# Two accumulators for the scattered expert outputs of a sixteen-image network, instead of one

## The chip, the cores and the metric

The kernel runs on one core of one Trainium2 chip. The core has five engines that work in parallel and wait for each other by semaphores: TensorE (PE in the profile, with its weight loads as PEld), VectorE (DVE), ScalarE (ACT), GpSimd (POOL) and SyncE (SP). SP, ACT and POOL also start transfers (DMAs), which all run on the same 16 DMA engines. The metric is the device time of one execution in microseconds (us), as the median of several runs.

## What is computed

A batch of 16 images of 128 channels and 32x32 pixels goes through a chain of blocks (a convolution block, linear attention, two attention layers, two feed-forward layers). The change is in the last one, a mixture of eight experts. There `x` is seen as 16,384 tokens of 128 channels. Eight rounds of row and column normalising give each token a gate for each expert; each of the 8 experts takes its best `m` = 128 tokens, multiplies them by its 128x128 matrix, and the results are added back at the places of the tokens:

```python
vals, idx = jax.lax.top_k(jnp.transpose(cg, (0, 2, 1)), m)      # 128 of 16384 tokens per expert
...
routed = xf[jnp.arange(h)[:, None, None], idx]
outputs = jnp.einsum('hmei,eio->hmeo', routed, experts)
outputs = outputs * gate_values[..., None]
...
s = jnp.zeros((N, o_dim), srcf.dtype).at[idxf].add(srcf)
c = jnp.zeros((N,), srcf.dtype).at[idxf].add(1.0)
return s / (c + 1.0)[:, None]
...
t = t + _L3_ffn_ref(_ln_t(t), L3_ffn_gate_w, L3_ffn_experts)
```

Two experts can choose the same token, so the additions of different experts to one row must not run over each other.

## The kernel before

The activations stay in the core's memory as `X`, 128 channels (partitions) by 16,384 tokens. The network is a row of phases, with a barrier of all engines after each. Two phases touch the change.

`phase_route` finds the tokens. Its SP part fills the accumulator `res` in device memory (16,384 rows of 128 float32, 8 MB) with zeros: 8 DMAs of 1 MB (line 2252), written `(t p) c -> p t c`, so that one partition of a DMA holds 16 rows that lie 128 rows apart, 512 bytes each. VectorE works through the routing in one chain of dependent steps; near its end line 2444 makes `ids`, the token number of each of the 128 picks of each expert (`tile_of * 128 + tok`). The zeros need only be there at the barrier after the phase.

`phase_experts` has four parts.

- Gather: POOL fetches the tokens of each expert with one indirect DMA each (line 2474, 8 DMAs).
- Experts: PE transposes them (line 2502) and multiplies by the expert's matrix (line 2507); VectorE scales each result by its weight into `give[:, e, :]` (line 2527, counted by `o_saved`).
- Scatter: POOL adds `give[:, e, :]` into the rows of `res` with an indirect DMA that accumulates (line 2481). Each waits for the landing of the one before (`added`, line 2480), since two experts may share a row.
- Read-back: SP waits for all eight scatters (line 2487), then loads `res` image by image (1,024 tokens, 512 KB, line 2492) into `rows[u]`, two buffers `u`. PE turns each 128x128 piece with a transpose into the banks `px[u][h]` (8 per image, line 2515), VectorE adds each half image to `X` (line 2533), and ACT writes the image to the output (line 2541). SP may load image b once the transposes of image b - 2 are done (`x_mm`, line 2491).

The helper `over` runs the 16 images as two straight steps, a loop, and two straight steps. Each engine issues its instructions in the order of the code; nothing reorders them.

Of the kernel before, what the change touches and what calls it, by code (L numbers as in the profile page):

```python
# [11 lines left out]
F32 = mybir.dt.float32  # L12
BF16 = mybir.dt.bfloat16
ALU = mybir.AluOpType
# [3 lines left out]
C = 128  # L18
B = 16
HW = 32  # L20
N = HW * HW
T = B * N
# [390 lines left out]
def wait_if(eng, sem, value):  # L413

    if not isinstance(value, int) or value > 0:
        eng.wait_ge(sem, value)
# [1748 lines left out]
E8 = 8  # L2165
ITERS = 8
TOP = N // E8
NT = T // C
CLIP = 1e-10


def phase_route(nc, K, D, Y, ids, ws):

# [3 lines left out]
    with Mem(nc, "sk") as m:  # L2179
# [63 lines left out]
        with nc.Block() as block:  # L2243
            @block.sync
            def _(sp):
                sp.wait_ge(const_ready, 1)
                for j in range(4):
                    sp.dma_start(gw[:, j, 32 * j:32 * j + E8], D["gate_w"]).then_inc(g_in, 16)

                sp.wait_ge(const_ready, 2)  # L2250
                for k in range(NT // 16):
                    sp.dma_start(D["res"][k * 16 * C:(k + 1) * 16 * C, :].rearrange("(t p) c -> p t c", p=C),
                                 zeros[:, :, :]).then_inc(zero_out, 16)
                sp.wait_ge(zero_out, 16 * (NT // 16))

            @block.gpsimd
            def _(g):
# [84 lines left out]
            def _(v):  # L2342
# [98 lines left out]
                for k in range(4):  # L2441
                    step(v.tensor_tensor(sel[:, 2 * k:2 * k + 2, :], pair[k][:, :, 0, :], bc_n(rank[:, 2 * k:2 * k + 2]), ALU.is_le))
                step(v.reduce_sum(tok[:, :], sel[:, :, :], AX.X))
                step(v.scalar_tensor_tensor(ids[:, :], tile_of[:, :], float(C), tok[:, :], ALU.mult, ALU.add))
                step(v.tensor_tensor(sel[:, :, :], token[:, :].rearrange("p (o n) -> p o n", o=1).to_broadcast([C, E8, C]),
                                     bc_n(tok[:, :]), ALU.is_equal))
                for k in range(4):
# [1 line left out]
                step(v.reduce_sum(ws[:, :], sel[:, :, :], AX.X))  # L2449


def phase_experts(nc, K, D, X, ids, ws):


    TI = N // C
    with Mem(nc, "ex") as m:
        ew = m.sb("ew", [C, E8, C])
        got = m.sb("got", [C, E8, C])
        gotT = m.sb("gotT", [C, E8, C])
        give = m.sb("give", [C, E8, C])  # L2460
        rows = [m.sb(f"rows{u}", [C, TI, C]) for u in range(2)]
        pt = [m.ps(f"pt{u}", [C, C]) for u in range(2)]
        po = [m.ps(f"po{u}", [C, C]) for u in range(2)]
        px = [[m.ps(f"px{u}{h}", [C, 4, C]) for h in range(2)] for u in range(2)]
        e_in, got_in = m.sem("e_in"), m.sem("got_in")
        t_ready, t_saved, o_mm, o_saved, added = (m.sem(x) for x in ("t_ready", "t_saved", "o_mm", "o_saved", "added"))
        rows_in = [m.sem("rows_in0"), m.sem("rows_in1")]
        out = [m.sem("out0"), m.sem("out1")]
        x_mm, x_ready = m.sem("x_mm"), m.sem("x_ready")
        with nc.Block() as block:  # L2470
            @block.gpsimd
            def _(g):
                for e in range(E8):
                    g.indirect_dma_start(got[:, e, :], None, D["tokens"], bass.IndirectOffsetOnAxis(ap=ids[:, e:e + 1], axis=0))\  # L2474
                     .then_inc(got_in, 16)
                for e in range(E8):
                    g.wait_ge(o_saved, e + 1)
                    if e:

                        g.wait_ge(added, 16 * e)  # L2480
                    g.indirect_dma_start(D["res"], bass.IndirectOffsetOnAxis(ap=ids[:, e:e + 1], axis=0), give[:, e, :], None,
                                         compute_op=ALU.add).then_inc(added, 16)

            @block.sync
            def _(sp):
                sp.dma_start(ew[:, :, :], D["experts"]).then_inc(e_in, 16)
                sp.wait_ge(added, 16 * E8)

                def step(b, u, last):

                    wait_if(sp, x_mm, 2 * b - 2)
                    sp.dma_start(rows[u][:, :, :], D["res"][bass.ds(b * N, N), :].rearrange("(t p) c -> p t c", p=C))\  # L2492
                      .then_inc(rows_in[u], 16)

                over(sp, B, step)

            @block.tensor
            def _(pe):
                for e in range(E8):
                    pe.wait_ge(got_in, 16 * E8)  # L2500
                    wait_if(pe, t_saved, e - 1)
                    pe.transpose(pt[e % 2][:, :], got[:, e, :], K["ident"][:, :]).then_inc(t_ready, 1)  # L2502
                pe.wait_ge(e_in, 16)
                for e in range(E8):
                    pe.wait_ge(t_saved, e + 1)
                    wait_if(pe, o_saved, e - 1)
                    pe.matmul(po[e % 2][:, :], gotT[:, e, :], ew[:, e, :], start=True, stop=True).then_inc(o_mm, 1)  # L2507

                def step(b, u, last):
                    pe.wait_ge(rows_in[u], 8 * (b - u) + 16)  # L2510
                    for h in range(2):

                        wait_if(pe, x_ready, 2 * b + h - 3)
                        for r in range(4):
                            done = pe.transpose(px[u][h][:, r, :], rows[u][:, 4 * h + r, :], K["ident"][:, :])  # L2515
                        done.then_inc(x_mm, 1)

                over(pe, B, step)

            @block.vector  # L2520
            def _(v):
                for e in range(E8):
                    v.wait_ge(t_ready, e + 1)
                    v.tensor_copy(gotT[:, e, :], pt[e % 2][:, :]).then_inc(t_saved, 1)  # L2524
                for e in range(E8):
                    v.wait_ge(o_mm, e + 1)
                    v.tensor_scalar(give[:, e, :], po[e % 2][:, :], ws[:, e:e + 1], None, ALU.mult).then_inc(o_saved, 1)  # L2527

                def step(b, u, last):
                    for h in range(2):  # L2530
                        v.wait_ge(x_mm, 2 * b + h + 1)
                        xb = X[:, bass.ds(b * N + h * CH, CH)]
                        v.tensor_tensor(xb, xb, px[u][h][:, :, :].rearrange("p r c -> p (r c)"), ALU.add).then_inc(x_ready, 1)  # L2533

                over(v, B, step)

            @block.scalar
            def _(a):
                def step(b, u, last):
                    a.wait_ge(x_ready, 2 * b + 2)  # L2540
                    a.dma_start(D["out"][bass.ds(b, 1)].rearrange("o c n -> c (o n)"), X[:, bass.ds(b * N, N)]).then_inc(out[u], 16)

                over(a, B, step)
                for u in range(2):
                    a.wait_ge(out[u], 16 * B // 2)


def build(nc, D):
    with ExitStack() as ctx:
        def sb(name, shape, dt=F32):  # L2550
            return ctx.enter_context(nc.sbuf_tensor(name, shape, dt))

        K = {"ident": sb("ident", [C, C]), "ones": sb("ones", [C, C]),
             "neghalf": sb("neghalf", [C, C]), "mask8": sb("mask8", [C, C]),
             "eps": sb("eps", [C, 4]), "negone": sb("negone", [C, 4]),
             "stats": sb("bnstats", [C, NCH, 6])}
        X = sb("X", [C, T])
        D["proj"] = nc.dram_tensor("proj", [C, T], F32).ap()
        D["qk"] = nc.dram_tensor("qk", [2, 3, C, T], BF16).ap()
        D["tokens"] = nc.dram_tensor("tokens", [T, C], F32).ap()  # L2560
        D["res"] = nc.dram_tensor("res", [T, C], F32).ap()
        D["u"] = nc.dram_tensor("u", [C, T // C, C + RVW], F32).ap()
        phase_constants(nc, K)
        phase_conv(nc, K, D, X)
        phase_linatt(nc, K, D, X)
        phase_linatt_norm(nc, K, D, X)
        phase_attn_prep(nc, K, D, X)
        phase_attn(nc, K, D, X)
        with Mem(nc, "ffn") as m:
            Y = m.sb("Y", [C, T])  # L2570
            wcol, b2w = m.sb("wcol", [C, FT, B]), m.sb("b2w", [C, B])
            phase_norm(nc, K, X, Y, "n2")
            phase_router(nc, K, D, Y, wcol, b2w)
            phase_ffn(nc, K, D, X, Y, wcol, b2w)
        with Mem(nc, "gqa") as m:
            Y = m.sb("Y", [C, T])
            phase_norm(nc, K, X, Y, "n3")
            phase_gqa(nc, K, D, X, Y)
        with Mem(nc, "moe") as m:
            Y = m.sb("Y", [C, T])  # L2580
            ids, ws = m.sb("ids", [C, E8], mybir.dt.int32), m.sb("ws", [C, E8])
            phase_norm(nc, K, X, Y, "n4", D["tokens"])
            phase_route(nc, K, D, Y, ids, ws)
            phase_experts(nc, K, D, X, ids, ws)


def layout(inputs):
# [59 lines left out]
```

## Time and profile before

| | us |
|---|---|
| median of 3 runs | 5307.86 (5302.34 to 5311.43) |
| the profiled execution, its own time | 5307.08 |
| its span in the trace | 5305.1 |
| first scatter starts | 5206.79 |
| last scatter landed, first load of `res` issued | 5238.73 |
| last addition to `X` ends | 5301.42 |
| end of the span | 5305.1 |

So the scatters take 31.9 us and the read-back with the output takes 66.4 us, both at the very end of the program, where nothing else runs beside them. Starts are in microseconds from the start of the span. A row of the timeline shows the start, the duration, the engine, the line, what is written and read, how many instructions are merged in the row, and in brackets how long the engine was idle before it and what ended that. A row of the windows view shows the stretch, its length, the busy time of PE, PEld, DVE, ACT and POOL with the number of their instructions, and then PEclk, the granted clock of TensorE, 1.00 for 2.4 GHz and 0.50 for 1.2 GHz; the last two are the mean busy share of the 16 DMA engines and what they moved in GB/s.

### The profile page before, as it was taken

Reading aid. Unit: us, or ns where it says so; the run is one execution under the profiler, and the core shown is the slowest. Engines: PE = TensorE matmul, PEld = TensorE weight load, DVE = VectorE, ACT = ScalarE, POOL = GpSimd, SP = SyncE. Lnnn points to the kernel's source line nnn. Section 1 sums busy time; section 2 is a strip of 40 time slices with the busy share of each in tenths; the row PEclk is TensorE's granted clock in tenths of the full one; section 3 lists DMA queues with packets and bytes.
Section 4 is the critical chain, followed back from the end, with each engine's and each line's share of the span. In section 5 each row is a group of like instructions: output and inputs, shape, how many; then the busy total and the mean of one; then the engine's idle time right before and its main releaser. Section 6 shows DMA issues by size and latency. Waiting matters only on the chain. (4 is left out here: it accounts for less than half of the span.)

```text
span 5305.1 us, 72474 instructions
## 1 busy us (share of the span) xinstructions
PE 4422.0 (83%) x21774; PEld 1678.8 (32%) x21775; DVE 3041.7 (57%) x5454; ACT 2105.6 (40%) x3845; POOL 1822.3 (34%) x1328
## 2 busy tenths in 40 slices
PE   5499999994699999999999999966999999565323
PEld 2133333332422222222222222223444444344222
DVE  4777777774687776767676677634000000567562
ACT  3311111114626665656565566653443344413100
POOL 1000000003727776767676777771000000303001
PEclk9799999996969999999999999987999999866655
DMA  1343344434722222322222222010000000213204
GB/s 68 73 101 88 88 103 95 90 69 159 257 37 30 32 32 30 41 31 30 31 36 31 37 31 32 7 48 35 0 0 0 0 0 0 99 44 124 78 0 138
DMA packets 208215, 295.49 MB, mean 56 GB/s; under 512 B 43943, under 2 KB 136109, under 8 KB 206525
## 3 DMA queue, kind: packets, MB, share of 16 engines
q1 hardware_dynamic: 179768, 256.87, 21.9%
q10 hardware_dynamic: 23808, 25.17, 1.3%
q0 software_dynamic: 4368, 10.07, 0.6%
q8 instruction: 142, 2.33, 0.2%
q14 instruction: 129, 1.06, 0.1%
HBM read 94.49 MB, written 69.73 MB: 31 GB/s over the span
## 5 line engine op out<-in xcount | busy, mean ns | idle before, releaser
L1578 DVE TENSOR_REDUCE at_mx<-at_side 128x1 f32<-128x512 f32 x2048 | 1295.0, 684 | 415.1 <-PE at_side L1481 404.2
L1652 ACT ACTIVATE at_P<-at_S 128x512 f32<-128x512 f32 x2048 | 1120.2, 599 | 749.5 <-PE at_S L1513 698.1
L1411 POOL TENSOR_TENSOR at_pairs<-at_P 128x2048 f32<-128x2048 f32 x256 | 1160.3, 4533 | 316.1 <-ACT at_P L1652 295.5
L1513 PE MATMUL at_S<-at_qo,at_ko 99*128 99x512 bf16 x2048 | 784.2, 387 | 76.0 <-ACT at_P L1652 76.0
L1481 PE MATMUL at_side<-at_ko,at_qo 96*128 96x512 bf16 x2048 | 788.8, 398 | 44.0 <-DMA at_ko<-qk 23.3
L1929 ACT ACTIVATE ff_hs<-ff_ph,ff_b 128x512 f32<-128x512 f32 x512 | 351.6, 687 | 524.0 <-PE ff_ph L1899 524.0
L1524 PE MATMUL at_num<-at_P,at_rvt 128*32 128x512 f32 x4096 | 550.1, 609 | 0.0
L1899 PE MATMUL ff_ph<-ffn_Y,ff_w 128*128 (+1 forms) x1024 | 524.3, 594 | 8.7 <-DMA ff_b<-in_b_dram 8.7
L1913 PE MATMUL ff_po<-ff_hs,ff_w2s 128*128 128x512 f32 x1024 | 522.5, 592 | 0.0
L616 PE MATMUL la_acc<-la_rep,la_wagg 128*32 128x512 f32 x4096 | 511.1, 606 | 1.2 <-DMA la_rep<-la_pad 1.2
L773 DVE SCALAR_TENSOR_TENSOR la_dwq<-la_pad,la_taps,la_dwq 128x1024 f32<-128x1024 f32 x384 | 491.7, 1280 | 7.2
L1948 DVE SCALAR_TENSOR_TENSOR X<-ff_po,ffn_b2w,X 128x512 f32 (+1 forms) x32 | 24.0, 751 | 822.3 <-PE ff_po L1913 822.3
L1513 PEld LDWEIGHTS at_S<-at_qo,at_ko 99*128 99x128 bf16 x2048 | 196.1, 97 | 884.0 <-ACT at_P L1652 684.2
L1008 POOL TENSOR_TENSOR n_ln_ab<-n_ln_mv,eps 128x4 f32<-128x4 f32 x96 | 19.1, 199 | 1201.8 <-DVE n_ln_mv L999 1199.9
L587 POOL DMA_DIRECT2D proj<-la_y x32 | 17.4, 543 | 993.5 <-ACT la_y L847 993.5
L1481 PEld LDWEIGHTS at_side<-at_ko,at_qo 96*128 96x128 bf16 x2048 | 201.3, 98 | 325.3 <-DVE at_mx L1578 136.5
L1535 PE MATMUL at_den<-at_pairs,ones 128*32 128x512 f32 x2048 | 277.1, 613 | 7.7 <-POOL at_pairs L1411 7.6
L1899 PEld LDWEIGHTS ff_ph<-ffn_Y,ff_w 128*128 128x128 f32 x1024 | 195.1, 191 | 254.2 <-issue 244.9
L1913 PEld LDWEIGHTS ff_po<-ff_hs,ff_w2s 128*128 128x128 f32 x1024 | 194.5, 190 | 245.0 <-issue 244.4
L1023 ACT ACTIVATE n_ln_xt<-n_ln_front,n_ln_ab 128x128 f32<-128x128 f32 x384 | 144.6, 456 | 102.7 <-POOL n_ln_ab L1014 92.1
L616 PEld LDWEIGHTS la_acc<-la_rep,la_wagg 128*32 128x32 f32 x4096 | 105.8, 108 | 246.5 <-issue 228.1
L831 ACT COPY la_agg<-la_acc 128x512 f32<-128x512 f32 x64 | 37.5, 587 | 343.1 <-PE la_acc L616 343.1
(409 smaller groups left out, 4601.0 us busy)
## 6 DMA issues: line engine op xcount, KB each, us to landing
la_rep<-la_pad SPq DMA_DIRECT2D x512, 162.2 KB, 3.6
qk<-ap_part SPq DMA_DIRECT2D x32, 768.0 KB, 3.7
at_qo<-qk SPq DMA_DIRECT2D x192, 128.0 KB, 4.6
at_ko<-qk SPq DMA_DIRECT2D x192, 128.0 KB, 7.7
n_ln_xs<-X SPq DMA_DIRECT2D x96, 256.0 KB, 2.3
u<-ap_us SPq DMA_DIRECT2D x32, 320.0 KB, 4.0
X<-in_x_dram SPq DMA_DIRECT2D x4, 2048.0 KB, 22.1
proj<-la_y POOLq DMA_DIRECT2D x32, 256.0 KB, 2.3
```

The costliest lines, as they stand in the source:

```text
L616: last = pe.matmul(acc[h][32 * j:32 * j + 32, :], wagg[:, p - 1, j, g, :], view[:, :, 0:HW], start=(g == 0), stop=(g == NG - 1))
L773: v.scalar_tensor_tensor(out, image, taps[:, t:t + 1], out, ALU.mult, ALU.add).then_inc(tap_done, 1)
L1411: g.tensor_tensor(pairs[i % 2][:, :, :], P[a][:, :, :], P[a + 1][:, :, :], ALU.add).then_inc(pair_done, 1)
L1481: return pe.matmul(side[bank][:, :], qo[1 - u][0:KQ, s, i * C:(i + 1) * C], ko[1 - u][0:KQ, s, h * CH:(h + 1) * CH], start=True, stop=True)
L1513: pe.matmul(S[n % RING][:, :], ko[u][:, h, j * C:(j + 1) * C], qo[u][:, h, half * CH:(half + 1) * CH], start=True, stop=True).then_inc(s_r ...
L1524: last = pe.matmul(num[32 * i:32 * i + 32, :], rvt[u][:, j, :], P[k % SLOTS][:, i, :], start=(j == 0), stop=(j == 7))
L1535: last = pe.matmul(den[32 * i:32 * i + 32, :], K["ones"][:, 0:32], pairs[(k // 2 - 1) % 2][:, i, :], start=(j == 0), stop=(j == 6))
L1578: v.reduce_max(mx[:, n // 2, n % 2:n % 2 + 1], side[bank][:, :], AX.X).then_inc(side_saved, 1)
L1652: a.activation(P[k % SLOTS][:, i, :], S[(4 * k + i) % RING][:, :], ACT.Exp).then_inc(p_ready, 1)
L1899: pe.matmul(ph[j % R][:, :], w1[:, f, :], Y[:, bass.ds(b * N + half * CH, CH)], start=True, stop=True).then_inc(h_mm, 1)
L1913: done = pe.matmul(po[half][:, :], w2s[u][:, f, :], hs[j % R][:, :], start=(f == 0), stop=(f == FT - 1)).then_inc(h_used, 1)
L1929: a.activation(hs[j % R][:, :], ph[j % R][:, :], ACT.Gelu, bias=b1[:, j % FT:j % FT + 1]).then_inc(h_ready, 1)
```

## The change

There are now two accumulators, `res` for the experts 0, 2, 4, 6 and `res1` for 1, 3, 5, 7. A scatter waits for the one two before it, on the same accumulator (`added[0]` and `added[1]`). Both accumulators are zeroed. The rows are laid out in another order in memory: token `tile * 128 + tok` lies in row `tok * 128 + tile`, so that the rows that one partition loads for an image (8 tiles) or zeroes in one DMA (16 tiles) lie side by side, 4 KB and 8 KB. VectorE makes these row numbers (`places`) with one more instruction. In the read-back both accumulators are loaded, transposed and added to `X`: per image two loads, 16 transposes and 4 additions where there were one, 8 and 2. There are still four banks `px`, now one for each accumulator and half image, so that they hold one image where they held two.

```diff
             for k in range(NT // 16):
-                sp.dma_start(D["res"][k * 16 * C:(k + 1) * 16 * C, :].rearrange("(t p) c -> p t c", p=C),
-                             zeros[:, :, :]).then_inc(zero_out, 16)
-            sp.wait_ge(zero_out, 16 * (NT // 16))
+                for chain in ("res", "res1"):
+                    sp.dma_start(D[chain].rearrange("(p t) c -> p t c", p=C)[:, 16 * k:16 * k + 16, :],
+                                 zeros[:, :, :]).then_inc(zero_out, 16)
+            sp.wait_ge(zero_out, 32 * (NT // 16))
...
             step(v.scalar_tensor_tensor(ids[:, :], tile_of[:, :], float(C), tok[:, :], ALU.mult, ALU.add))
+            step(v.scalar_tensor_tensor(places[:, :], tok[:, :], float(NT), tile_of[:, :], ALU.mult, ALU.add))
...
-        rows = [m.sb(f"rows{u}", [C, TI, C]) for u in range(2)]
+        rows = [[m.sb(f"rows{k}{u}", [C, TI, C]) for u in range(2)] for k in range(2)]
-        px = [[m.ps(f"px{u}{h}", [C, 4, C]) for h in range(2)] for u in range(2)]
+        px = [[m.ps(f"px{k}{h}", [C, 4, C]) for h in range(2)] for k in range(2)]
...
                 for e in range(E8):
                     g.wait_ge(o_saved, e + 1)
-                    if e:
-                        g.wait_ge(added, 16 * e)
-                    g.indirect_dma_start(D["res"], bass.IndirectOffsetOnAxis(ap=ids[:, e:e + 1], axis=0), give[:, e, :], None,
-                                         compute_op=ALU.add).then_inc(added, 16)
+                    if e >= 2:
+                        g.wait_ge(added[e % 2], 16 * (e // 2))
+                    g.indirect_dma_start(chains[e % 2], bass.IndirectOffsetOnAxis(ap=places[:, e:e + 1], axis=0), give[:, e, :], None,
+                                         compute_op=ALU.add).then_inc(added[e % 2], 16)
...
-                    wait_if(sp, x_mm, 2 * b - 2)
-                    sp.dma_start(rows[u][:, :, :], D["res"][bass.ds(b * N, N), :].rearrange("(t p) c -> p t c", p=C))\
-                      .then_inc(rows_in[u], 16)
+                    wait_if(sp, x_mm, 4 * b - 4)
+                    for k in range(2):
+                        sp.dma_start(rows[k][u][:, :, :], chains[k].rearrange("(p t) c -> p t c", p=C)[:, bass.ds(b * TI, TI), :])\
+                          .then_inc(rows_in[u], 16)
...
-                    pe.wait_ge(rows_in[u], 8 * (b - u) + 16)
+                    pe.wait_ge(rows_in[u], 16 * (b - u) + 32)
                     for h in range(2):
-                        wait_if(pe, x_ready, 2 * b + h - 3)
-                        for r in range(4):
-                            done = pe.transpose(px[u][h][:, r, :], rows[u][:, 4 * h + r, :], K["ident"][:, :])
-                        done.then_inc(x_mm, 1)
+                        for k in range(2):
+                            wait_if(pe, x_ready, 4 * b + 2 * h + k - 3)
+                            for r in range(4):
+                                done = pe.transpose(px[k][h][:, r, :], rows[k][u][:, 4 * h + r, :], K["ident"][:, :])
+                            done.then_inc(x_mm, 1)
...
                     for h in range(2):
-                        v.wait_ge(x_mm, 2 * b + h + 1)
                         xb = X[:, bass.ds(b * N + h * CH, CH)]
-                        v.tensor_tensor(xb, xb, px[u][h][:, :, :].rearrange("p r c -> p (r c)"), ALU.add).then_inc(x_ready, 1)
+                        for k in range(2):
+                            v.wait_ge(x_mm, 4 * b + 2 * h + k + 1)
+                            if k:
+                                v.wait_ge(x_ready, 4 * b + 2 * h + 1)
+                            v.tensor_tensor(xb, xb, px[k][h][:, :, :].rearrange("p r c -> p (r c)"), ALU.add).then_inc(x_ready, 1)
```

On POOL, at the gathers and scatters in `phase_experts`, the instructions stand as follows (semaphore names in brackets are those of the first phase that used the same semaphore: `conv_pool` is `o_saved`, `conv_vec` is `added` before and `added[0]` after, `conv_act` is `added[1]`):

```order
-L2474 DMA ex_got<-tokens,moe_ids 128x128 x8
-L2481 DMA res<-ex_give,moe_ids 16384x128 [waits conv_pool]
-L2481 DMA res<-ex_give,moe_ids 16384x128 [waits conv_vec,conv_pool] x7
...
+L2478 DMA ex_got<-tokens,moe_ids 128x128 x8
+L2485 DMA res<-ex_give,moe_places 16384x128 [waits conv_pool] x2
+L2485 DMA res<-ex_give,moe_places 16384x128 [waits conv_vec,conv_pool]
+L2485 DMA res<-ex_give,moe_places 16384x128 [waits conv_act,conv_pool]
```

The second scatter no longer waits for the first, and from the third on the waits alternate between the two semaphores; the eight are still issued by one engine, one after the other.

On PE, inside the loop of the read-back, one image (of the two in the loop's body) stands as follows (`conv_pe` and `conv_coef1_ready` are the landings of the loads, `conv_v1_ready` before and `conv_v2_ready` after are `x_ready`, the additions that free a bank):

```order
 L416 ISA [waits conv_pe]
-L2515 MATMUL ex_px<-ident,ex_rows 128x128 [waits conv_v1_ready]
-L2515 MATMUL ex_px<-ident,ex_rows 128x128 x3
-L416 REGISTER_ALU
-L2515 MATMUL ex_px<-ident,ex_rows 128x128 [waits conv_v1_ready]
-L2515 MATMUL ex_px<-ident,ex_rows 128x128 x3
+L2522 MATMUL ex_px<-ident,ex_rows 128x128 [waits conv_v2_ready]
+L2522 MATMUL ex_px<-ident,ex_rows 128x128 x3
+L416 REGISTER_ALU
+L2522 MATMUL ex_px<-ident,ex_rows 128x128 [waits conv_v2_ready]
+L2522 MATMUL ex_px<-ident,ex_rows 128x128 x3
+L416 REGISTER_ALU
```

Two groups of four transposes have become four groups, each with its wait for a bank, behind one wait for both loads of the image.

## Rows read from the trace of the kernel before

**Rows 1.** The timeline: first two scatters, the last, and the loads of `res`.

```profile
5206.79 1.63 POOL L2481 DMA_INDIRECT res<-ex_give,moe_ids  x1 [6.20 <-DVE ex_give L2527]
5211.02 1.56 POOL L2481 DMA_INDIRECT res<-ex_give,moe_ids  x1 [2.60 <-DVE ex_give L2527]
...
5235.41 1.55 POOL L2481 DMA_INDIRECT res<-ex_give,moe_ids  x1 [2.52 <-DMA res<-ex_give,moe_ids]
5238.73 53.95 SPq L2492 DMA_DIRECT2D ex_rows<-res  x16
```

**Rows 2.** The chain that ended last: start, duration, what; two scatters.

```profile
5226.49 0.71 issue
5227.21 3.38 DMA res<-ex_give,moe_ids
5230.59 0.02 issue
...
5230.63 0.71 issue
5231.34 3.32 DMA res<-ex_give,moe_ids
```

**Rows 3.** The timeline: two gathers on POOL, and PE's wait for the last.

```profile
5198.41 0.94 POOL L2474 DMA_INDIRECT ex_got<-tokens,moe_ids  x1 [0.30 <-issue]
5199.66 0.94 POOL L2474 DMA_INDIRECT ex_got<-tokens,moe_ids  x1 [0.30 <-issue]
5202.22 0.29 PEld L2502 LDWEIGHTS ex_pt<-ident,ex_got 128*128 128x128 f32 x2 [21.33 <-DMA ex_got<-tokens,moe_ids]
```

**Rows 4.** The loads of `res`, all 16: issue times, and issue to landing.

```profile
L2492 SPq DMA_DIRECT2D ex_rows<-res x16: 372/378/576, 5238.7 to 5292.3; - x16
...
DMA to landing us min/median/max: 3.8/4.6/7.6
```

**Rows 5.** The chain that ended last: one load and its transposes, and the end.

```profile
5244.71 4.38 DMA ex_rows<-res
5249.08 0.13 issue
5249.22 1.98 PE ex_px L2515 x8
...
5292.30 6.37 DMA ex_rows<-res
5298.68 0.04 issue
5298.72 1.99 PE ex_px L2515 x8
5300.71 0.02 issue
5300.73 0.69 DVE X L2533
```

**Rows 6.** The timeline of the read-back: 16 transposes in a row, and one addition.

```profile
5276.87 3.67 PE L2515 MATMUL ex_px<-ident,ex_rows 128*128 128x128 f32 x16 [2.92 <-DMA ex_rows<-res]
5278.98 0.69 DVE L2533 TENSOR_TENSOR X<-X,ex_px 128x512 f32 x1 [0.17 <-PE ex_px L2515]
```

**Rows 7.** Windows: input load, load of `proj`, LayerNorm (three), zeroing, routing, read-back.

```profile
20.00:30.00 10.00, 0.00 (x0) 0.00 (x0) 9.21 (x20) 1.16 (x1) 0.00 (x0) 1.00 1.02 408
1220.40:1222.40 2.00, 0.00 (x0) 0.00 (x0) 0.00 (x0) 0.00 (x0) 0.52 (x1) 0.50 1.00 414
4852.00:4912.00 60.00, 40.16 (x209) 32.23 (x210) 49.95 (x238) 39.70 (x106) 43.24 (x110) 0.74 0.67 221
4856.00:4860.00 4.00, 2.29 (x18) 1.71 (x16) 3.80 (x19) 2.49 (x8) 3.48 (x10) 1.00 0.85 293
4868.00:4872.00 4.00, 3.62 (x16) 3.14 (x16) 2.96 (x16) 2.51 (x8) 1.96 (x7) 0.50 0.57 192
4929.00:4932.00 3.00, 3.00 (x7) 1.25 (x6) 0.00 (x0) 0.00 (x0) 0.00 (x0) 0.72 1.02 283
4960.00:5189.00 229.00, 51.12 (x316) 37.80 (x316) 169.45 (x271) 0.21 (x1) 0.00 (x0) 0.53 0.00 0
5244.00:5292.00 48.00, 24.89 (x107) 20.69 (x105) 17.98 (x27) 0.00 (x0) 0.00 (x0) 0.54 0.79 264
```

**Rows 8.** The loads of `proj`, 1 MB each, line 885: issue to landing.

```profile
DMA to landing us min/median/max: 4.7/4.9/7.9
```

**Rows 9.** The timeline of the LayerNorm: four transposes at either granted clock.

```profile
4857.15 0.60 PE L976 MATMUL n_ln_front<-ident,n_ln_xs 128*128 128x128 f32 x4
4869.01 1.06 PE L976 MATMUL n_ln_front<-ident,n_ln_xs 128*128 128x128 f32 x4
```

**Rows 10.** The timeline at the end of the routing: `ids` and the step behind it.

```profile
5184.42 0.17 DVE L2444 SCALAR_TENSOR_TENSOR moe_ids<-sk_tile_of,sk_tok 128x8 int32<-128x8 f32 x1
5184.62 1.23 DVE L2445 TENSOR_TENSOR sk_sel<-sk_token,sk_tok 128x1024 f32<-128x1024 f32 x1
```

More of the change, by code:

```diff
@@ L2169, with phase_route @@
 CLIP = 1e-10
-def phase_route(nc, K, D, Y, ids, ws):
+def phase_route(nc, K, D, Y, ids, places, ws):
     with Mem(nc, "sk") as m:
@@ L2449, in _, with phase_experts @@
                 step(v.reduce_sum(ws[:, :], sel[:, :, :], AX.X))
-def phase_experts(nc, K, D, X, ids, ws):
+def phase_experts(nc, K, D, X, ids, places, ws):
     TI = N // C
@@ L2460, in phase_experts @@
         give = m.sb("give", [C, E8, C])
-        rows = [m.sb(f"rows{u}", [C, TI, C]) for u in range(2)]
+        rows = [[m.sb(f"rows{k}{u}", [C, TI, C]) for u in range(2)] for k in range(2)]
         pt = [m.ps(f"pt{u}", [C, C]) for u in range(2)]
         po = [m.ps(f"po{u}", [C, C]) for u in range(2)]
-        px = [[m.ps(f"px{u}{h}", [C, 4, C]) for h in range(2)] for u in range(2)]
+        px = [[m.ps(f"px{k}{h}", [C, 4, C]) for h in range(2)] for k in range(2)]
         e_in, got_in = m.sem("e_in"), m.sem("got_in")
-        t_ready, t_saved, o_mm, o_saved, added = (m.sem(x) for x in ("t_ready", "t_saved", "o_mm", "o_saved", "added"))
-        rows_in = [m.sem("rows_in0"), m.sem("rows_in1")]
+        t_ready, t_saved, o_mm, o_saved = (m.sem(x) for x in ("t_ready", "t_saved", "o_mm", "o_saved"))
+        added = [m.sem("added0"), m.sem("added1")]
+        chains = (D["res"], D["res1"])
+        rows_in = [m.sem(f"rows_in{u}") for u in range(2)]
         out = [m.sem("out0"), m.sem("out1")]
@@ L2486, in _ @@
                 sp.dma_start(ew[:, :, :], D["experts"]).then_inc(e_in, 16)
-                sp.wait_ge(added, 16 * E8)
+                for k in range(2):
+                    sp.wait_ge(added[k], 8 * E8)
                 def step(b, u, last):
-                    wait_if(sp, x_mm, 2 * b - 2)
-                    sp.dma_start(rows[u][:, :, :], D["res"][bass.ds(b * N, N), :].rearrange("(t p) c -> p t c", p=C))\
-                      .then_inc(rows_in[u], 16)
+                    wait_if(sp, x_mm, 4 * b - 4)
+                    for k in range(2):
+                        sp.dma_start(rows[k][u][:, :, :], chains[k].rearrange("(p t) c -> p t c", p=C)[:, bass.ds(b * TI, TI), :])\
+                          .then_inc(rows_in[u], 16)
                 over(sp, B, step)
@@ L2530, in step @@
                     for h in range(2):
-                        v.wait_ge(x_mm, 2 * b + h + 1)
                         xb = X[:, bass.ds(b * N + h * CH, CH)]
-                        v.tensor_tensor(xb, xb, px[u][h][:, :, :].rearrange("p r c -> p (r c)"), ALU.add).then_inc(x_ready, 1)
+                        for k in range(2):
+                            v.wait_ge(x_mm, 4 * b + 2 * h + k + 1)
+                            if k:
+                                v.wait_ge(x_ready, 4 * b + 2 * h + 1)
+                            v.tensor_tensor(xb, xb, px[k][h][:, :, :].rearrange("p r c -> p (r c)"), ALU.add).then_inc(x_ready, 1)
                 over(v, B, step)
@@ L2539, in step @@
                 def step(b, u, last):
-                    a.wait_ge(x_ready, 2 * b + 2)
+                    a.wait_ge(x_ready, 4 * b + 4)
                     a.dma_start(D["out"][bass.ds(b, 1)].rearrange("o c n -> c (o n)"), X[:, bass.ds(b * N, N)]).then_inc(out[u], 16)
@@ L2561, in build @@
         D["res"] = nc.dram_tensor("res", [T, C], F32).ap()
+        D["res1"] = nc.dram_tensor("res1", [T, C], F32).ap()
         D["u"] = nc.dram_tensor("u", [C, T // C, C + RVW], F32).ap()
@@ L2580, in build @@
             Y = m.sb("Y", [C, T])
-            ids, ws = m.sb("ids", [C, E8], mybir.dt.int32), m.sb("ws", [C, E8])
+            ids, places = (m.sb(x, [C, E8], mybir.dt.int32) for x in ("ids", "places"))
+            ws = m.sb("ws", [C, E8])
             phase_norm(nc, K, X, Y, "n4", D["tokens"])
-            phase_route(nc, K, D, Y, ids, ws)
-            phase_experts(nc, K, D, X, ids, ws)
+            phase_route(nc, K, D, Y, ids, places, ws)
+            phase_experts(nc, K, D, X, ids, places, ws)
 def layout(inputs):
```

## The prediction

> **What bounds the kernel now.** I read the timeline of the end first, since the change touches nothing else on the path. It shows two stretches in which almost everything waits. In the first, eight scatters start 4.1 us apart and wait for each other's landing: from 5206.79 to 5238.73, 31.9 us [rows 1]. The chain of waits splits one step: 0.71 us on POOL before the scatter begins, then 3.38 us until it has landed, of which POOL itself is busy for 1.55 us [rows 1, 2]. In the second, the read-back, the chain goes from a load of `res` to its eight transposes and from there to the next load into the same buffer [rows 5]: two buffers, so two images per round. The first and the fifteenth load are seven rounds apart and the last load is issued right behind the fifteenth; 16 issues lie in 5292.3 - 5238.7 = 53.6 us [rows 4], 7.6 us a round. Of the round, the transposes take 1.98 us and the hand-overs 0.3 us [rows 5], so the landing takes 5.3 us on average, while the load that found the DMA engines empty took 3.8 us [rows 4]: 1.5 us are contention with the other buffer's load and the output. The DMA engines are busy for 0.79 of the stretch, TensorE for 24.89 of 48 us at a granted clock of 0.54 [rows 7]. So this stretch is bound by latency (load, then transposes), with the DMA engines near behind.
>
> **The scatters.** Two chains on one issuing engine. The second scatter needs nothing but POOL: it can start 1.55 us plus the gap of an issue that waits for nothing after the first. Gathers issued in a row have a gap of 0.30 us [rows 3], so 1.85 us. The third waits for the first to land and starts 4.07 us after it, as now; POOL has been free since 3.4 us. So even scatters start at 0, 4.07, 8.14 and 12.2 us, the last odd one at 14.1, and it has landed 3.35 us later, at 17.4. Saved: 31.9 - 17.4 = 14.5 us. If each issue costs the 0.71 us of rows 2 whether it waited or not, a pair takes 2 x 2.26 = 4.5 us and POOL sets the pace: 3 x 4.5 + 2.26 + 3.35 = 19.2, saved 12.8. I take **14 saved**, near the upper end. That two scatters in flight do not slow each other down is read from the gathers: they start 1.25 us apart and the last one still lands within 2.6 us of its start [rows 3]; the DMA engines are nearly idle there. The experts' results come faster than the scatters take them: by 5211.02 POOL waits only for the scatter before.
>
> **places.** One more instruction in VectorE's chain, as small as `ids`: 0.17 us and 0.03 to the next step [rows 10]: **+0.2 us**. The order in which rows are scattered changes, not their number or size.
>
> **Zeroing.** Twice the bytes, in pieces of 8 KB. The 512-byte pieces of before saturate the DMA engines at 283 GB/s [rows 7]; at that pace 16.8 MB take 59 us, at the 408 of the input load 41 us. Behind it lie 229 us of routing with the DMA share at 0.00 [rows 7], and only the barrier at its end needs the zeros: **0**. Without that cover it would be 12 to 30 us.
>
> **The read-back, the price of the second accumulator.** Three things change in a round.
>
> The landing. An image is now 1 MB in 4 KB pieces, at a distance of 64 KB from partition to partition. The nearest row is the load of `proj`, 1 MB as well and at the same distance, in 8 KB pieces: 4.7 us when nothing is in its way [rows 8], against 3.8 for 512 KB in 512-byte pieces. The doubling costs only 0.9 us because larger pieces go faster: `proj` ran at 414 GB/s and the input, in 4 KB pieces, at 408, both with the DMA engines full, the 512-byte zeroes at 283 [rows 7]. For contention I keep 1.5 us as the low end; scaled by what is in the way (a load and a write, 1.85 + 1.28 us of full DMA engines before, 2.57 + 1.28 after, each 524 or 1049 KB by those rates) it is 1.9. I take 1.7: landing 6.4 us.
>
> The Trainium skill ("DMA: Bandwidth & Descriptors", Specifications) puts the smallest transfer that reaches line rate at 512 bytes. By that the new layout would make nothing faster, and the sum would be that of the third rival; the zeroing at a full DMA share and 283 GB/s [rows 7] speaks against the page, so I do not use it.
>
> The transposes. 16 in a row take 3.67 us at the lower clock [rows 6]. At the higher clock a group of four takes 0.60 us, at the lower 1.06 [rows 9]; 16 would take about 1.9 us. This is the term that I know least. VectorE adds 4 x (0.69 + 0.17) = 3.4 us per image [rows 6], in step with PE at the lower clock; the smaller ring of banks holds one image, and is empty again while the next load lands, so I give it 0. Its 6.9 us a round lie beside the load.
>
> The clock. Before, PE is busy for 0.52 of the stretch and gets 0.54 [rows 7]. With 2 x 3.67 us in a round of 10.4 it would be busy for 0.71 at the lower clock. The LayerNorm stage, which is mostly transposes of the same shape, has PE busy for 0.67 and gets 0.74 on average, in turns of 0.50 and 1.00 [rows 7]. I take the same: half of the rounds at either clock.
>
> The Trainium skill ("TensorE: Matmul & The Clock Gate", Part 4: PE-mode transpose) says that the full clock does not engage for transposes, as they do not count as activity. By it, the second rival would be the forecast. The stretch from 4856 to 4860 holds transposes only (lines 976 and 984) and has a clock of 1.00 [rows 7]; the trace disagrees.
>
> Round at the lower clock: 6.4 + 3.67 + 0.3 = 10.4 us; seven take 72.6, 19.0 more than now. At the higher: 6.4 + 1.9 + 0.3 = 8.6; 60.2, 6.6 more. The DMA engines alone need 2 x (2.57 + 1.28) = 7.7 a round, so they are no bound yet. Outside the seven rounds, the first load lands 0.9 later, the last (6.37 us now, [rows 5]) too, and the last image's transposes take 1.7 more at the lower clock and nothing at the higher. Sums: +22.5 and +8.4 us; the mean, **+15**. With 1.5 and 1.9 for contention the ends are +7 and +24.
>
> **Sum.** -14 + 0.2 + 15 = +1.2 us. On the profiled execution's 5307.08 this gives 5308.3; the median of the runs lies 0.8 above that execution, so **5309**. Ends of the terms: -14.5 + 0.2 + 7 = -7 and -12.8 + 0.2 + 24 = +11, that is 5300.5 to 5319. About 0.2%, 10.6 us, is what a measurement of this kernel can tell from no change; the runs of before alone spread over 9 us.
>
> **Rivals.**
> First, *the higher clock holds*: the read-back costs 8.4 and the change wins 5.4 us: 5302.5. For it: longer stretches of transposes; full clock came in LayerNorm behind stretches of PE work at 0.9 busy (3.62 of 4 us, [rows 7]). Against: 7 us without PE work in every round.
> Second, on the slower side, *the clock stays low in the read-back*: every round pays the 3.67 us twice over, +22.5, together +8.7: 5317. For it: 0.54 before, and 3-us gaps in front of each load. It decides from about 9 rounds in 10 at the lower clock on.
> Third, *larger pieces are no faster when they are read 64 KB apart while outputs are written*: a load then has 3.7 us of transfer for 1.85 now; it lands in 3.8 + 1.85 + 1.7 = 7.4 us, a round takes 10.5 at the mean of the clocks, and the read-back +24 with its ends: +10, 5318, and 5325 at the lower clock. For it: nothing in the trace reads 4 KB pieces at that distance. Against: rows 7 and 8 on `proj`.
> Fourth, *the two scatters do not overlap*, or the change does not do what it says: if the second one's data wait for the first one's (1.8 us of its landing lie behind POOL's 1.55), a pair takes 5.9 us, and only 7.5 us are saved: +7.7, 5316. Against: the gathers.
>
> **Chances.** Forecast 0.45 (5303 to 5315), first rival 0.15, second 0.20, third 0.10, fourth 0.10. Above 5318.5 lie some 0.02 of the forecast, 0.06 of the second, 0.07 of the third and 0.04 of the fourth: slower 0.19. Below 5297.3 lie 0.01 of the forecast and 0.05 of the first: faster 0.06. Same: 0.75. The range takes in both ends and the centres of all rivals and leaves out the tails of the first and third: 5298 to 5322.
>
> **What would show it.** In the trace after: scatters that start in pairs, about 1.9 us and then 2.2 us apart, and a last landing some 17.5 us after the first start; `zeros` at about 400 GB/s; the 16 image steps 4.3 to 5.2 us apart, with a granted clock of about 0.75; a landing of some 6.4 us from the first of an image's two loads. The forecast is wrong if the clock stays at one of its levels, if loads reach less than 350 GB/s with the DMA engines full, or if odd scatters land more than 4 us after their start.

## The result

The changed kernel takes 5325.1 us (median of 8 runs, 5319.8 to 5328.0) against 5309.8 us of the kernel before (8 runs, 5302.3 to 5314.6): a ratio of 1.003, interval 1.0019 to 1.0040, some 15 us slower. I had forecast 5309 and a range up to 5322; the time lies outside.

The profiled execution has a span of 5326.4 us, 21.3 more than before. The timeline shows the scatters and the first loads (compare [rows 1]):

```profile
5214.57 1.63 POOL L2485 DMA_INDIRECT res<-ex_give,moe_places  x1 [6.26 <-DVE ex_give L2534]
5216.51 1.56 POOL L2485 DMA_INDIRECT res<-ex_give,moe_places  x1 [0.31 <-issue]
5218.75 1.55 POOL L2485 DMA_INDIRECT res<-ex_give,moe_places  x1 [0.68 <-DVE ex_give L2534]
...
5228.80 1.55 POOL L2485 DMA_INDIRECT res<-ex_give,moe_places  x1 [0.41 <-issue]
5232.14 81.09 SPq L2498 DMA_DIRECT2D ex_rows<-res  x32
```

From the first scatter to the first load are now 17.6 us instead of 31.9: the pairs start 1.94 and 2.24 us apart, as foretold. From the first load to the end of the span are 94.3 us instead of 66.4. The rest of the 21.3 us has nothing to do with the change: the zeroing starts 4.7 us later already, and from there to `ids` it takes 259.5 us instead of 256.7, a time that four further traces of these two kernels show too (259.4 to 259.6), two of them of the kernel before. So 4.7 + 2.8 + 0.2 - 14.4 + 27.9 = 21.2.

The chain that ended last, in the read-back (start, duration, what; compare [rows 5]):

```profile
5232.53 5.00 DMA ex_rows<-res
5237.53 0.05 issue
5237.58 3.69 PE ex_px L2522 x16
...
5241.88 6.75 DMA ex_rows<-res
5248.63 0.13 issue
5248.77 3.69 PE ex_px L2522 x16
...
5273.37 8.22 DMA ex_rows<-res
...
5281.71 6.32 PE ex_px L2522 x32
...
5288.63 7.74 DMA ex_rows<-res
```

Each row of the DMA begins with the second load of the image; the first was issued 0.4 us before. Landings of 5.0 to 8.2 us alternate with mostly 3.7 us of transposes, once with those of both images in a row (x32). Windows of the same trace (columns as in [rows 7]): the read-back, the first loads alone, and the zeroing:

```profile
5241.00:5312.00 71.00, 39.39 (x210) 35.48 (x208) 34.97 (x53) 0.00 (x0) 0.00 (x0) 0.69 0.86 288
5235.00:5238.00 3.00, 0.42 (x2) 0.43 (x3) 0.00 (x0) 0.00 (x0) 0.00 (x0) 0.50 1.02 412
4940.00:4946.00 6.00, 6.00 (x19) 2.84 (x18) 0.29 (x1) 0.58 (x1) 0.00 (x0) 1.00 1.01 416
```

The 4 KB pieces at 64 KB distance do run at 412 GB/s, the zeroing in 8 KB pieces at 416 (283 before), and the clock of 0.69 is about the 0.74 that I took. None of the rivals that I named is it.

The same row of the first loads of the kernel before, which I had not read:

```profile
5241.00:5243.00 2.00, 0.45 (x2) 0.45 (x3) 0.00 (x0) 0.00 (x0) 0.00 (x0) 0.50 1.15 347
```

Reads in 512-byte pieces ran at 347 GB/s, not at the 283 of the writes by which I had priced them.

### The profile page after: what moved, and what is told of

The parts are those of the page before. It is cut to its first block and busy times, and to the rows that moved or that the text cites. A ratio compares the mean times of both kernels' runs of the same rounds, so it can differ in the third digit from the quotient of the medians.

```text
span 5326.4 us, 72869 instructions
## 1 busy us (share of the span) xinstructions
PE 4466.1 (84%) x21903; PEld 1710.7 (32%) x21903; DVE 3065.3 (58%) x5487; ACT 2104.9 (40%) x3845; POOL 1822.2 (34%) x1328
## 5 line engine op out<-in xcount | busy, mean ns | idle before, releaser
L587 POOL DMA_DIRECT2D proj<-la_y x32 | 17.4, 544 | 996.0 <-ACT la_y L847 996.0
```

## The experiments

All of them are read in the same two places: S, from the start of the first scatter to the first load of the read-back, and R, from that load to the end of the span. The execution time of a single run is not used, since what lies ahead of the change moves the first scatter, and with it the end, by up to 10 us from run to run.

**The stage itself, three traces each.** The kernels as they are.

> The kernel before, a second look at the read-back (66.4 us in the first). If the first was a usual draw, 64 to 69; if its length depends on how loads and output writes happen to meet, as 4.4 against 7.6 us of landing in one chain suggest, anything from 62 to 72.

> The kernel before, a third look at its read-back: 64 to 69 us if it is steady, 62 to 72 if it depends on how loads and output writes meet.

> The changed kernel as it is, a second look at the stage: is a round of 11.4 us (79.5 us for the seven rounds from the second to the last load pair) its usual size or a draw of the clock? If usual: read-back 92 to 97 us. If a draw: below 88. Scatters 17.4 to 17.6 us.

> The changed kernel, a third look at its read-back (94.3 and 87.5 us so far). The medians of the timed runs lie 15.3 us apart, the scatters save 14.4: read-backs should differ by 29 or so on average, so 90 to 97 is expected; below 88 would leave some of the 15.3 us unexplained.

R before: 66.4, 67.0, 62.2, mean 65.2. R changed: 94.3, 87.5, 94.3, mean 92.0. So the read-back costs 26.9 us more, with a spread of 4.8 us before and 6.8 us after; S is 31.6 and 17.5 on average. Together 26.9 - 14.1 + 0.2 = +13.0, which fits the 15.3 of the timed medians. One trace of each could have given anything from 20 to 32 us. Most kernels below have a single trace; differences in R of less than 7 us are not told apart.

**What the added loads and the added transposes cost alone.** In the first kernel both loads stay, with one set of transposes and additions:

```diff
-                    wait_if(sp, x_mm, 4 * b - 4)
+                    wait_if(sp, x_mm, 2 * b - 2)
...
-                        for k in range(2):
-                            wait_if(pe, x_ready, 4 * b + 2 * h + k - 3)
+                        wait_if(pe, x_ready, 2 * b + h - 3)
...
-                                done = pe.transpose(px[k][h][:, r, :], rows[k][u][:, 4 * h + r, :], K["ident"][:, :])
+                            done = pe.transpose(px[u][h][:, r, :], rows[0][u][:, 4 * h + r, :], K["ident"][:, :])
```

> The changed kernel, both accumulators loaded, but only the first is transposed and added: the odd experts' part is left out of the output. Prices the second load alone. Theory that transfers carry the cost of 28 us: 88 to 92 us of read-back. Theory that the second set of transposes at the lower clock carries it: 72 to 76. If both add up, as in a round of landing plus transposes: landing 7.5, transposes 2.0, hand-overs 0.3, a round of 9.8 and about 82 us.

In the second there is one load, and its rows are transposed and added twice:

```diff
-                    for k in range(2):
+                    for k in range(1):
                         sp.dma_start(rows[k][u][:, :, :], ...
...
-                    pe.wait_ge(rows_in[u], 16 * (b - u) + 32)
+                    pe.wait_ge(rows_in[u], 8 * (b - u) + 16)
...
-                                done = pe.transpose(px[k][h][:, r, :], rows[k][u][:, 4 * h + r, :], K["ident"][:, :])
+                                done = pe.transpose(px[k][h][:, r, :], rows[0][u][:, 4 * h + r, :], K["ident"][:, :])
```

> The changed kernel, but only the first accumulator is loaded, and its rows are transposed and added twice: the output holds the even experts' part twice and the odd ones' not at all. Prices the second set of transposes and additions alone. Transfers carry the cost: 66 to 69 us. Transposes carry it: 85 or more. Both add up: landing 5.0, transposes 3.5, hand-overs 0.3, a round of 8.8 and 76 us. Granted clock of the stretch above 0.6 if a larger busy share of PE raises it.

R was 84.3 and 65.2 us. The first kernel also has the old ring of banks, which holds two images. The middle of the read-back, two loads first, two transposes second:

```profile
5235.00:5298.00 63.00, 24.67 (x102) 19.47 (x100) 17.50 (x26) 0.00 (x0) 0.00 (x0) 0.50 0.93 316
```

```profile
5239.00:5283.00 44.00, 26.88 (x196) 23.76 (x195) 32.10 (x50) 0.00 (x0) 0.00 (x0) 0.92 0.88 290
```

The second load alone brings 19 us over the mean of before, the second set of transposes and additions nothing that can be seen. Both kernels have the new order of rows; against one accumulator in that order (62.8, next experiment) it is 21.5 and 2.4. With twice the transposes the clock was 0.92, and image by image 16 transposes took 2.3 us where 8 had taken 1.9. So the theory that the transfers carry the cost holds (its 66 to 69 us for the second kernel, and 4 us less than its 88 to 92 for the first); "both add up" missed the second kernel by 11 us. The two costs alone make 84, the changed kernel 92. In it the clock is lower (0.67 to 0.73) and 16 transposes take 3.0 us instead of 2.3, which over seven rounds would be 5 of these 8 us. That is worked out, not tested, and 8 us is little more than the spread.

**The order of the rows.** One accumulator in the new order, and two in the old one; of each only the load is shown, the zeroing and the row numbers of the scatters go with it:

```diff
...
-                    sp.dma_start(rows[u][:, :, :], D["res"][bass.ds(b * N, N), :].rearrange("(t p) c -> p t c", p=C))\
+                    sp.dma_start(rows[u][:, :, :], D["res"].rearrange("(p t) c -> p t c", p=C)[:, bass.ds(b * TI, TI), :])\
...
```

> One accumulator, one chain of scatters, but rows in the new order (places), so that loads come in 4 KB pieces. Read-back from the first load's issue to the end of the span: 66.4 us before. If larger pieces are read at 410 GB/s instead of 346, a load of 512 KB loses 0.25 us, a round 0.3 to 0.4: 63 to 64 us. As I had priced them in the prediction (283 to 408 GB/s) a round loses 0.8: 60 us. If pieces 64 KB apart are slow beside writes: 67 us or more. Scatters unchanged, 4.07 us apart.

```diff
...
-                        sp.dma_start(rows[k][u][:, :, :], chains[k].rearrange("(p t) c -> p t c", p=C)[:, bass.ds(b * TI, TI), :])\
+                        sp.dma_start(rows[k][u][:, :, :], chains[k][bass.ds(b * N, N), :].rearrange("(t p) c -> p t c", p=C))\
...
```

> The change with the rows in the old order: two accumulators, two chains, 512-byte pieces. Read-back 94.3 us in the changed kernel. Reads at 346 instead of 410 GB/s: 0.5 us more an image's landing, a round of 12.0 to 12.3 instead of 11.4: 99 to 101 us. As priced in the prediction: 105 us. If pieces do not matter, or 4 KB pieces 64 KB apart are the slow ones: 94 us or less. Scatters in pairs, 17.5 us in all.

R 62.8, which lies inside the spread of before, and 101.0, outside that of the changed kernel (87.5 to 94.3). So the new order is a help of 7 to 13 us where an image is 1 MB, and too small to show where it is 512 KB. The third rival has it the wrong way round.

**What the output's writes do to the loads.** Both kernels with only 8 of the 1024 columns of an image written, the rest left out:

```diff
-                    a.dma_start(D["out"][bass.ds(b, 1)].rearrange("o c n -> c (o n)"), X[:, bass.ds(b * N, N)])...
+                    a.dma_start(D["out"][bass.ds(b, 1)].rearrange("o c n -> c (o n)")[:, 0:8], X[:, bass.ds(b * N, 8)])...
```

> The kernel before, but of each image only 8 of 1024 columns are written to the output (the rest is left out). In the changed kernel leaving the output out takes 18.8 us off (94.3 to 75.5). If the output's writes stretch a landing by their own transfer (1.28 us an image at 410 GB/s) whatever the load: the same 18 us here, 48. If the stretch grows with the load that it meets, as my term for contention did not have it: about 1 us a round less, 58 to 60.

> The changed kernel, but of each image only 8 of 1024 columns are written to the output (the rest is left out). Shows what the output's transfers cost the loads. If reads alone run at 410 GB/s, two loads need 5.1 us of DMA engines a round pair of images; landing 5.4, transposes 3, hand-overs 0.3: a round of 8.7 and 70 us of read-back, against 94.3. If loads of 4 KB pieces 64 KB apart are slow by themselves, it stays above 80.

R was 53.6 before and 75.5 in the changed kernel. The loads of the chain that ended last, kernel before without output, then the changed one:

```profile
5253.82 3.85 DMA ex_rows<-res
...
5259.94 3.83 DMA ex_rows<-res
...
5266.05 3.82 DMA ex_rows<-res
```

```profile
5239.57 4.96 DMA ex_rows<-res
5244.66 5.17 PE ex_px L2522 x32
...
5250.43 7.01 DMA ex_rows<-res
...
5261.86 4.75 DMA ex_rows<-res
```

Before, without output, every load in the chain but one lands in 3.8 to 3.9 us, as fast as the one with nothing in its way. From the sixth image on these loads are issued 2.3 to 3.2 us apart, so that each meets little of the other image's; the one exception, 4.6 us, was issued 1.5 us behind it. From the second image's load to the last is 44 us, 6.3 a round, which is 3.9 + 2.0 + 0.3 and the first, slower rounds. In the changed kernel it is 63 us, 9.1 a round, with landings of 5.8 us on average there against 5.1 to 5.4 for the first image. Again it is a few that are long: 13 of the 16 pairs landed in 5.1 to 5.6 us, three in 6.9 to 7.5, and these three were issued 0.9 to 1.8 us behind the other image's. Leaving the output out takes 11.6 us off the mean of before and 16.5 off that of the changed kernel. Of the two expectations for the kernel before (48 us, and 58 to 60) neither came out, and whether the output's stretch grows with the load can't be told from 5 us of difference.

That the other image's load has a part is plainer with the output. Two pairs of neighbouring loads in the kernel before, one issued 1.6 us apart, one 4.9 (first and last issue, then the shorter and the longer landing):

```profile
L2492 SPq DMA_DIRECT2D ex_rows<-res x2: 378/378/378, 5267.5 to 5269.1; - x2
...
DMA to landing us min/median/max: 4.3/6.0/7.6
```

```profile
L2492 SPq DMA_DIRECT2D ex_rows<-res x2: 372/372/372, 5274.1 to 5279.0; - x2
...
DMA to landing us min/median/max: 4.1/4.2/4.3
```

So it goes in all three traces of the kernel before, from the third image on: the 11 loads that were issued at most 2.5 us behind the other image's landed in 6.3 to 7.8 us, 7.0 on average; the other 31 in 4.5 on average, 27 of them in less than 4.9. The two traces with R of 66.4 and 67.0 have five such loads each, the one with 62.2 has one. In the three traces of the changed kernel 23 pairs were issued at most 5.7 us behind the other image's and landed in 8.3 us on average, and 19 later, in 6.3.

The same bytes, with all writes behind the last addition:

```diff
-                    a.wait_ge(x_ready, 4 * b + 4)
+                    a.wait_ge(x_ready, 4 * B)
```

> The changed kernel with all 16 output writes issued only after the last addition. Same bytes, no reads beside writes. If mixing reads and writes makes the DMA engines slower per byte (338 GB/s at full share in the mix, 410 in reads alone), the reads take about 70 us, the writes 8.4 MB at 410 GB/s 20 us and 2 us of latency: about 92 us together, with DMA engines at 410 GB/s when full. If the mix costs nothing per byte, reads and writes one after the other take over 100 us.

R 100.5: 77.4 us until the writes begin, 23.1 for them, at 403 GB/s in their middle. Taking the two apart gains nothing, as expected for the case that reads beside writes cost no more per byte; the runs with four buffers show that directly.

**Clock, and the issue of two loads.** Eight further matmuls behind the transposes of each image:

```diff
...
+                    for r in range(8):
+                        pe.matmul(pt[r % 2][:, :], got[:, 0, :], K["ident"][:, :], start=True, stop=True)
...
```

> The changed kernel with 8 extra 128x128 matmuls on PE behind the transposes of each image (their result is not used), to keep the clock up. If the lower clock carries what I missed: clock above 0.9, read-back 94.3 less 16 x (3.1 - 2.0) x one half, about 85. If the landings carry it: 92 or more, since the transposes of one image only lie in the way once a round.

The clock rose to 0.94 in the middle of the read-back, and R was 87.4, at the lower end of the changed kernel's own spread and 4.6 under its mean. That is no difference that one trace can claim. Image by image the 16 transposes took 2.3 us instead of 3.0, which over seven rounds is 5 us, while the landings stayed at 7.3 us. A full clock would thus give back some 5 us, an estimate from these rows, and leaves the larger part where it is.

One tensor in which the rows of the two accumulators alternate, so that an image is one load of 1 MB:

```diff
...
-                    for k in range(2):
-                        sp.dma_start(rows[k][u][:, :, :], chains[k].rearrange("(p t) c -> p t c", p=C)[:, bass.ds(b * TI, TI), :])\
+                    sp.dma_start(rows[u][:, :, :, :], D["res"].rearrange("(p t) k c -> p t k c", p=C)[:, bass.ds(b * TI, TI), :, :])\
...
```

> Two chains of scatters into one tensor in which the rows of both accumulators alternate, so that an image is one load of 1 MB in 8 KB pieces instead of two loads of 512 KB. If the second issue and start belong to the landing (5.4 us for the first image's pair, 4.7 for the single load of proj): the first landing 4.7 to 4.9, a round 0.7 us less than the changed kernel's 10.6 to 11.4, read-back 82 to 89. If the landing is set by what else is on the DMA engines: no change, 87 to 94. Scatters 17.5 us.

The first image landed in 4.7 us, as the load of `proj` does [rows 8], against 5.1 to 5.4 with two loads; R was 86.5, inside the expected band but also within a microsecond of the lowest trace of the changed kernel. That the issue costs some tenths per landing is shown for the first image only.

**More loads in flight.** Four image buffers instead of two, with two accumulators, with one in the new order, and with one in the old order:

```diff
-        rows = [[m.sb(f"rows{k}{u}", [C, TI, C]) for u in range(2)] for k in range(2)]
+        rows = [[m.sb(f"rows{k}{u}", [C, TI, C]) for u in range(4)] for k in range(2)]
...
-                    wait_if(sp, x_mm, 4 * b - 4)
+                    wait_if(sp, x_mm, 4 * b - 12)
...
-                over(sp, B, step)
+                over(sp, B, step, 4)
```

> The changed kernel with four image buffers for the loads instead of two. If latency plus transposes set the pace, the read-back falls to about 70 us and the kernel to 5302. If the DMA engines are the bound at 338 GB/s, 25.2 MB need 74.5 us, read-back about 81, kernel about 5312. If the engines are already full at two buffers: no change, 5325.

> One accumulator and one chain of scatters with the new row order and four image buffers. DMA engines the bound at 338 GB/s: 16.8 MB in 50 us, read-back about 56 against 66.4 and 62.8 (two buffers, same layout), the kernel at 5300. Latency still the bound: 62, 5306. It should be faster than both kernels of the case.

> The kernel before (one accumulator, 512-byte pieces) with four image buffers. With 4 KB pieces four buffers gave 45.9 us at 416 GB/s. If 512-byte reads cost the engines more when they are full (346 GB/s alone): 8.4 MB in 24.2 us and 8.4 MB of writes in 20.4, 44.6 plus 5: 50 us. If the size of the pieces does not matter once enough is in flight: 46.

R was 69.2, 45.9 and 49.5 us. The middle of the read-back, in this order:

```profile
5240.00:5280.00 40.00, 24.23 (x178) 21.71 (x176) 29.22 (x45) 0.00 (x0) 0.00 (x0) 0.90 1.02 411
```

```profile
5257.00:5279.00 22.00, 14.46 (x73) 11.83 (x71) 11.66 (x19) 0.00 (x0) 0.00 (x0) 0.66 1.02 416
```

```profile
5250.00:5276.00 26.00, 12.87 (x76) 10.92 (x74) 12.93 (x20) 0.00 (x0) 0.00 (x0) 0.76 1.06 371
```

With four buffers the DMA engines are full, reads and writes mixed, at 411 to 416 GB/s (371 with 512-byte reads); with two the changed kernel moved 288. My first two expectations here took 338 GB/s (274 divided by the busy share of 0.81) for the limit of the mix, and what they built on it was 10 to 12 us too high. The other case of the first one, that with two buffers latency and transposes set the pace (70 us and 5302), came out, and so did the 50 us of the last. The busy share counts time in which the engines move little: in the first microseconds of the read-back the trace has shares of 0.6 to 1.1 at 82 to 164 GB/s.

Timed against 5309.0 of before beside them (16 runs): two accumulators and four buffers 5302.1 us (10 runs), 0.9986 of before (0.9976 to 0.9996); one accumulator, new order, four buffers **5292.8 us** (7 runs), 0.9971 (0.9959 to 0.9982). The latter beats both kernels. With full engines the second accumulator's 8.4 MB cost 23.3 us of read-back (69.2 - 45.9; 20.4 at 411 GB/s) and its scatters save 14, which agrees with the 9.3 us between the timed medians: it does not pay there either.

## Why the prediction was wrong

**Right.** The scatters: 17.4 us forecast for the pairs, 17.5 measured, the gap 0.30 us behind an issue that waits for nothing, and no slowing of two in flight (landing 3.3 us as before). I booked 14, and the three traces of either kernel give 14.1. `places`: 0.2. The zeroing stayed hidden; it took until about 4974 of the 5192 at which `ids` is made. The larger pieces at 64 KB distance: 412 GB/s. The clock: half and half forecast with 0.74 in mind, 0.67 to 0.73 measured over the read-back, transposes of 3.0 us per image instead of 2.8. The extra additions cost nothing that shows. That the clock rises in a stretch of nothing but transposes was shown again by the kernel with one load and two sets of them (0.92 over 44 us, where before had 0.54): the Trainium skill's statement ("TensorE: Matmul & The Clock Gate", Part 4: PE-mode transpose) that the full clock does not engage for them is not what this kernel does.

**Wrong: the landing of an image.** The step that failed is "I take 1.7: landing 6.4 us". In the second of the two buffers, which holds the last image and so ends the kernel, rounds of the changed kernel were 11.3, 10.5 and 11.4 us long, 11.1 on average, against the 9.5 that my two cases have as their mean. Read image by image, that is a landing of 7.6 us, 3.1 of transposes and 0.4 of hand-overs and waiting for TensorE. The 1.2 us that the landing took longer than 6.4, seven times, are 8 of the 12 us by which the read-back was forecast too short (26.9 against 15); the transposes (3.1 against 2.8) are 2 more, and about 1 comes from the rounds of before, which are 7.5 in three traces where I had 7.6.

Of the 1.2 us, 0.5 are the pair of loads alone: 5.2 us, not 4.7, as two loads start later than the one of `proj`. The other 0.7 are contention: 2.4 us where I took 1.7. I had scaled the 1.5 us of before by bytes, as if every load met the same traffic. The traces of before show a mixture instead: 7.0 us for the loads issued at most 2.5 us behind the other image's, 4.5 for the rest. Loads that take longer would overlap more; that is the likely reason why scaling by bytes fell short, and not shown by itself. Without the output the landing in this buffer was 5.8 us in the changed kernel and 4.1 before, so most of the contention goes away with the output. But the loads of before are then also spaced more evenly, and the two parts can't be priced one by one from these runs.

**Wrong as well: the price of 512-byte reads.** I took 283 GB/s from the zeroing, which writes. Reads of this size went at 347, in the window of the kernel before that is shown above. The new order thus gave the reads less than I thought, though the landing of 3.8 that I built on was measured and held. With 347 my own rule would have scaled the 1.5 us to 2.1 instead of 1.9 (3.85 against 2.79 us of full engines), nearer to the 2.4. A small misreading beside it: the last load of before was issued 2.4 us behind the fifteenth, not right behind it, so 7.6 us is the round of the second buffer alone.

**Too narrow: the range.** The rival of the low clock and that of slow pieces each reached 5317 to 5325, but the ends of the contention term were only 0.4 us apart, one rule applied with two factors. And one trace of a stage that itself spreads over 5 to 7 us carried the whole sum.

Still open: whether the nearness of the other image's load is by itself what makes a landing long. It goes with the long landings in both kernels (7.0 against 4.5 us before, 8.3 against 6.3 after), but hardly in the kernel with two loads and one set of transposes (7.8 us up to a distance of 5.7 us, 7.4 beyond). Images whose transposes follow each other directly (the x32 row) send their next loads off together; no run here forced or prevented that with the output in place.

## What to carry to other kernels

In this ring of two buffers the round is landing plus processing, and in the traces of both kernels a landing is longer when the other buffer's load was issued shortly before it; price a doubled load from a run or a row in which the neighbour's load is in the way too, not by scaling a wait. Ask first whether the DMA engines are full by their GB/s against the best stretch of the same trace, not by their busy share: 0.79 at 264 GB/s looked nearly full, and the same pieces ran at 371 with four buffers, larger ones at 411 to 416. Two more buffers, with the rows in the new order, took 16 us off the kernel where the second accumulator added 15. A second accumulator in memory pays only if what is read back for it (8.4 MB, 20 us here) costs less than the waits that it removes (14 us).

## What the runs showed of the hardware

Reads in 512-byte pieces ran at 347 GB/s and writes of the same size at 283; in 4 and 8 KB pieces both ran at 403 to 416, and a full mix of both at 411 to 416 (371 with 512-byte reads). Two accumulating scatters in flight, issued 1.9 us apart by one engine, landed as fast as one (3.3 us). A second set of 128 transposes in the read-back took no time that shows: the granted clock was 0.92 instead of 0.54, and 16 transposes took 2.3 us where 8 had taken 1.9. The busy share of the DMA engines says little about what they move: 0.86 went with 288 GB/s, 1.02 with 411.
